# Row maxima of an attention unit: merged by one VectorE instruction, transposed in fp32, split into two fp16 parts behind the transpose

## What is computed

```python
xn = layernorm(x)
q, k, v = split(xn @ W_attn + b_attn)          # 16 heads of 16 channels
q, k = rope(q), rope(k)                        # here: over the head axis, 16 angles
att = softmax(where(causal, q @ k.T / 4, -inf))
s = (att @ v) @ W_proj + b_proj
h = silu(xn @ w_gate.T / 127) * (xn @ w_up.T / 127)
out = x + s * silu(h @ w_down.T / 127)
```

## Time and profile before

| | |
|---|---|
| median of 3 runs | 1229.83 us (1229.42 to 1235.92) |
| span of the profiled execution, first to last instruction | 1225.2 us |
| PE / DVE / ACT / POOL busy | 1124.7 / 1039.1 / 891.3 / 771.0 us |
| mean granted clock of PE | 0.993 of full speed |

### The profile page before, as it was taken

The page is one execution under the profiler, slowest core; times in us unless marked ns, Lnnn a source line. Parts: engine busy times, 40 slices in busy tenths (PEclk is TensorE's granted clock), DMA queues, the critical chain, the costliest instruction groups (busy, mean ns, idle before and its releaser), DMA issues.

```text
span 1225.2 us, 27668 instructions
## 1 busy us (share of the span) xinstructions
PE 1124.7 (92%) x9484; PEld 455.5 (37%) x9484; DVE 1039.1 (85%) x3124; ACT 891.3 (73%) x1708; POOL 771.0 (63%) x943
## 2 busy tenths in 40 slices
PE   3789989999999999999899999999999998999996
PEld 2223423434343443434334342333434343343433
DVE  6789889988989889989899888898898998989832
ACT  4457777777777777777677777777777786878774
POOL 3537445595837948298564966469483894737672
PEclk9989999999999999999999999999999999999999
DMA  6250042403242150611425033431516115240201
GB/s 174 74 147 12 12 123 76 120 28 114 54 146 57 28 150 22 169 29 53 125 71 133 23 99 68 121 83 28 141 32 171 30 32 146 69 93 18 62 2 52
DMA packets 71281, 97.51 MB, mean 80 GB/s; under 512 B 18398, under 2 KB 44388, under 8 KB 71140
## 3 DMA queue, kind: packets, MB, share of 16 engines
q1 hardware_dynamic: 71072, 95.73, 28.2%
q10 hardware_dynamic: 68, 0.01, 0.0%
HBM read 52.76 MB, written 34.47 MB: 71 GB/s over the span
## 4 chain that ended last, share of the span: by engine, by line
PE 50%; POOL 20%; DVE 14%; issue 6%; ACT 6%; DMA 2%; SPq 1%; POOLq 0%; DVEq 0%; ACTq 0%
PE ring L931 25%; PE acc L922 11%; PE st L871 7%; PE ring L898 5%; POOL xn L579 5%; POOL hf L1629 4%; DVE ring L1294 4%; POOL pexp L1599 3%; ACT pexp L1129 3%; DVE mx_a L1298 2%; POOL hT L1638 1%; DVE parts L1356 1%; POOL hT L1633 1%; POOL yn L1648 1%; PE ring L941 1%
## 5 line engine op out<-in xcount | busy, mean ns | idle before, releaser
L1129 ACT ACTIVATE pexp<-st 128x512 f32<-128x512 f32 x1152 | 624.1, 598 | 139.1 <-PE st L871 136.4
L1294 DVE CUSTOM_DVE_ANT_0 ring<-ring,tri 128x512 f32<-128x512 f32 (+3 forms) x1024 | 470.2, 522 | 40.5 <-PE ring L898 39.6
L1599 POOL TENSOR_SCALAR_AFFINE_SELECT pexp<-pexp 128x512 f32<-128x512 f32 x256 | 158.0, 635 | 341.8 <-ACT pexp L1129 250.8
L1298 DVE TENSOR_REDUCE mx_a<-ring 128x1 f32<-128x512 f32 x512 | 326.9, 682 | 28.1 <-PE ring L898 26.2
L922 PE MATMUL acc<-pexp,v_pad 128*17 128x512 f32 (+3 forms) x3072 | 304.3, 491 | 16.7 <-POOL pexp L1599 14.5
L898 PE MATMUL ring<-k_st,q_st 56*128 56x512 f16 (+4 forms) x1536 | 237.6, 326 | 32.9 <-DVE parts L1356 11.4
L871 PE MATMUL st<-q_st,k_st 58*128 58x512 f16 (+3 forms) x1536 | 234.8, 332 | 6.6 <-ACT pexp L1129 3.4
L871 PEld LDWEIGHTS st<-q_st,k_st 58*128 58x128 f16 x1536 | 61.9, 93 | 275.9 <-ACT pexp L1129 175.7
L1629 POOL TENSOR_TENSOR hf<-ga,ups 128x512 f32<-128x512 f32 x96 | 121.8, 1272 | 10.3 <-DVE ga L1365 8.8
L922 PEld LDWEIGHTS acc<-pexp,v_pad 128*17 128x17 f32 x3072 | 61.4, 96 | 154.6 <-issue 119.6
L1638 POOL TENSOR_TENSOR hT<-hf,hT 128x512 f16<-128x512 f32 x96 | 110.8, 1158 | 6.7
(11 more groups left out here) (155 smaller groups left out, 1430.6 us busy)
## 6 DMA issues: line engine op xcount, KB each, us to landing
parts_scratch<-parts SPq DMA_DIRECT2D x32, 512.0 KB, 3.0
q_st<-parts_scratch SPq DMA_DIRECT2D x62, 192.0 KB, 3.9
k_st<-parts_scratch SPq DMA_DIRECT2D x62, 192.0 KB, 4.4
parts_scratch<-parts SPq DMA_DIRECT2D x32, 256.0 KB, 3.6
xo<-in_x SPq DMA_DIRECT2D x32, 256.0 KB, 3.2
out<-xo SPq DMA_DIRECT2D x32, 256.0 KB, 2.3
xn<-in_x SPq DMA_DIRECT2D x7, 1024.0 KB, 8.1
yn<-yT SPq DMA_DIRECT2D x224, 32.0 KB
```

The lines of the kernel that those rows point to most:

```text
L1129: nc.scalar.activation(pexp[:, GH * (n % NSET) + j, :], st[:, (GH * n + j) % NST, :], ACT.Exp, scale=1.0 / (QK_SCALE * np.sqrt(D))).then_i ...
L1294: top_ = nc.vector.tensor_tensor_reduce(out=src, in0=src, in1=tri[:, CH - w:CH], scale=1.0, scalar=NEG, op0=ALU.add, op1=ALU.max, accum_ou ...
L1298: top_ = nc.vector.reduce_max(dst, src, AX.X)
L1599: nc.gpsimd.affine_select(out=t, in_=t, compare_op=ALU.is_ge, fill=0.0, base=0, pattern=[[0, GH], [1, P]], channel_multiplier=-1).then_inc ...
```

## The change

The pieces of a row's maximum now lie side by side in one tile, `mx_s`, whose second column POOL fills once with -3e38 in the prologue. One reduce over pairs (L1309 of the changed kernel) writes 32 fp32 maxima into `mx_m`. PE transposes these 32 columns in fp32. ACT copies the 32 rows out of PSUM with the scale -1/32768 to fp16, the high part (L1207), and then DVE forms the low part from the same bank and ACT's result (L1371), which frees the bank. SP's four DMAs take their rows from the new layout of `mT`. The fp16 identity and its two POOL instructions are gone.

```diff
@@ LAG @@
-    "vector": {"TX": 0, "QK": 0, "UPG": 0, "DN": 0, "FT": 0, "YT": 0, "LNS": 0, "BP": 0, "YR": 1},
+    "vector": {"TX": 0, "QK": 0, "UPG": 0, "DN": 0, "FT": 0, "YT": 0, "LNS": 0, "BP": 0, "YR": 1, "MT": 0},
@@ rows_of_maxima, issued by SP @@
-                    first = 2 * TT * (2 * a + part)
+                    first = 2 * TT * a
...
-                                  mT[first:first + 2 * TT, :]).then_inc(mrow_in[g], 16)
+                                  mT[first:first + 2 * TT, part, :]).then_inc(mrow_in[g], 16)
@@ PE, task MT @@
-                    pe.wait_ge(mp_chain, 3 * BY["MT"].at(kind, i, t))
+                    pe.wait_ge(mx_ready, BY["MT"].at(kind, i, t))
                     dst, ready = take(kind, i, t)
-                    nc.tensor.transpose(dst[0:2 * GH * TT, :].bitcast(fp16)[:, 0:P],
-                                        mx_p[:, :, :, :, :].rearrange("p a s j t -> p (a s j t)"), ident16[:, :])\
-                        .then_inc(ready, 1)
+                    nc.tensor.transpose(dst[0:GH * TT, 0:P], mx_m[:, :], ident[:, :]).then_inc(ready, 1)
@@ ACT, task MT @@
-                    nc.scalar.activation(mT[:, :], src[0:2 * GH * TT, :].bitcast(fp16)[:, 0:P], ACT.Copy)\
-                        .then_inc(ring_free[b], 1)
+                    nc.scalar.activation(mT[:, 0, :], src[0:GH * TT, 0:P], ACT.Copy, scale=-1.0 / M_UNIT)\
+                        .then_inc(mt_high, 1)
@@ DVE, split_maxima @@
                 wait_done(dve, *last_max(kind, i, t), 1)
-                nc.vector.tensor_tensor(m[:, :, :, 4:8], m[:, :, :, 4:8], mx_b[:, par, :, :, :], ALU.max)\
-                    .then_inc(mp_chain, 1)
-                dve.wait_ge(mp_chain, base + 1)
...
-                nc.vector.tensor_scalar(mx_p[:, :, 0, :, :], m, -1.0 / M_UNIT, None, ALU.mult).then_inc(mp_chain, 1)
-                dve.wait_ge(mp_chain, base + 2)
-                nc.vector.scalar_tensor_tensor(out=mx_p[:, :, 1, :, :], in0=m, scalar=-1.0 / M_UNIT,
-                                               in1=mx_p[:, :, 0, :, :], op0=ALU.mult,
-                                               op1=ALU.subtract).then_inc(mp_chain, 1)
+                nc.vector.tensor_reduce(mx_m[:, :].rearrange("p (r o) -> p r o", o=1),
+                                        mx_s[:, par, :, :, :].rearrange("p r t s -> p (r t) s"), AX.X, ALU.max)\
+                    .then_inc(mx_ready, 1)
@@ DVE, task MT @@
+                if t[0] == "MT":
+
+                    dve.wait_ge(mt_high, BY["MT"].at(kind, i, t))
+                    nc.vector.scalar_tensor_tensor(out=mT[:, 1, :], in0=src[0:GH * TT, 0:P], scalar=-1.0 / M_UNIT,
+                                                   in1=mT[:, 0, :], op0=ALU.mult, op1=ALU.subtract)\
+                        .then_inc(ring_free[b], 1)
@@ POOL, prologue @@
+                pool.memset(mx_s[:, :, :, :, :], NEG).then_inc(mx_clear, 1)
...
-                pool.memset(ident16[:, :], 0.0).then_inc(const0, 1)
...
-                pool.affine_select(out=ident16[:, :], in_=ident16[:, :], compare_op=ALU.not_equal, fill=1.0, base=0,
-                                   pattern=[[-1, P]], channel_multiplier=1).then_inc(const_ready, 1)
```

More of the change, by code:

```diff
@@ L423, in build_program @@
         ident = sb("ident", [P, P], fp32)
-        ident16 = sb("ident16", [P, P], fp16)
         tri = sb("tri", [P, CH], fp32)
@@ L444, in build_program @@
         yrec = sb("yrec", [P, 4, 4 * GH], fp32)
[L445 to L448, removed]
+        mx_s = sb("mx_s", [P, 2, GH, TT, 2], fp32)
+        mx_m = sb("mx_m", [P, GH * TT], fp32)
+        mT = sb("mT", [GH * TT, 2, P], fp16)
         hT = sb("hT", [P, 2, HID // P, CH], fp16)
@@ L524, in build_program @@
         stack_in = [sem(f"stack_in{g}") for g in range(GROUPS)]
-        mp_chain = sem("mp_chain")
+        mx_clear = sem("mx_clear")
+        mx_ready = sem("mx_ready")
+        mt_high = sem("mt_high")
         mrow_in = [sem(f"mrow_in{g}") for g in range(GROUPS)]
@@ L1285, in max_take @@
                     dve.wait_ge(tri_ready, 1)
+                    dve.wait_ge(mx_clear, 1)
                 for a in range(2):
@@ L1290, in max_take @@
                     for t, k0, w, p in found:
-                        dst = mx_b[:, par, a, p, t - 4:t - 3] if k0 else mx_a[:, par, a, p, t:t + 1]
+                        dst = mx_s[:, par, 2 * a + p, t, (k0 > 0):(k0 > 0) + 1]
                         src = ring[:, b, at:at + w]
@@ L1304, in split_maxima @@
                 par = t[1] % 2
-                base = 3 * (BY["MT"].at(kind, i, t) - 1)
-                m = mx_a[:, par, :, :, :]
                 wait_done(dve, *last_max(kind, i, t), 1)
-                nc.vector.tensor_tensor(m[:, :, :, 4:8], m[:, :, :, 4:8], mx_b[:, par, :, :, :], ALU.max)\
-                    .then_inc(mp_chain, 1)
-                dve.wait_ge(mp_chain, base + 1)
                 if kind != "pro":
                     wait_ready(dve, *mt_before(kind, i, t))
-                nc.vector.tensor_scalar(mx_p[:, :, 0, :, :], m, -1.0 / M_UNIT, None, ALU.mult).then_inc(mp_chain, 1)
-                dve.wait_ge(mp_chain, base + 2)
-                nc.vector.scalar_tensor_tensor(out=mx_p[:, :, 1, :, :], in0=m, scalar=-1.0 / M_UNIT,
-                                               in1=mx_p[:, :, 0, :, :], op0=ALU.mult,
-                                               op1=ALU.subtract).then_inc(mp_chain, 1)
+                nc.vector.tensor_reduce(mx_m[:, :].rearrange("p (r o) -> p r o", o=1),
+                                        mx_s[:, par, :, :, :].rearrange("p r t s -> p (r t) s"), AX.X, ALU.max)\
+                    .then_inc(mx_ready, 1)
             def stats(kind, i, p):
@@ L1696, in prologue @@
                 pool.memset(hf[0:64, 1, :], float(np.uint32(0x78007800).view(np.float32))).then_inc(k_const, 1)
-                pool.wait_ge(const0, 5)
+                pool.wait_ge(const0, 4)
                 for p in range(2):
```

## The result

| | before | changed |
|---|---|---|
| median of 6 runs each | 1229.62 us (1225.03 to 1235.92) | 1216.45 us (1214.25 to 1222.60) |
| ratio, 95% interval | | 0.9901 (0.9877 to 0.9924) |
| span of the profiled execution | 1225.2 us | 1215.5 us |

The changed kernel is faster by 1.0%, some 12 us. The forecast was 8.6 us and 1221.2, with a range of 1214.5 to 1230.5. The direction, the range and the place of the gain were right. The gain was larger than forecast: 1216.45 lies at the very edge of the forecast's own 1216 to 1225, and under the 1217.8 that the prediction gave for added work that costs nothing.

A forecast was written before the change was run, and what follows sets the result against it. PE (92% busy, 50% of the chain) bounds the kernel, so DVE gains count only where PE waits for DVE. -13.2 + 1.0 + 2.4 + 1.2 = -8.6 us, from 1229.8 to 1221.2; range 1214.5 to 1230.5.

The forecast's parts named there:

- The three instructions take turns with POOL: Slots 24 and 25: three small DVE instructions alternate with POOL's large ones, holding DVE 3.06 us; the reduce takes 0.22.
- -13.2 in slots 24 and 25: PE's wait at L898 for `parts` goes, 11.4 us, plus 6 x 0.30 us of idling in the products behind.
- DVE's wait for ACT in slot 25: Before L1371 DVE idles 0.9 us for ACT's copy; taken as no loss, at most 2.8 us.
- the rival that ended slower: L1371 waits for ACT in slots 7, 16 and 34, 24 times at about 1.1 us: 1246 us; chance 0.06.
- +1.0 for L1371 in slots 7, 16 and 34: L1371 delays DVE's maxima behind it by 0.2 to 0.3 us; between none and 6 us, taken as 1.
- +2.4 for the DMAs: SP issues the maxima's DMAs 0.85 us later; four uncovered places cost 0.6 us each, eight at slot 9 nothing.
- +1.2 in the prologue: DVE waits for ACT's copy and does L1371 before its next maxima, delaying PE's first scores: cost 1.2 us.
- The sum: -13.2 + 1.0 + 2.4 + 1.2 = -8.6 us on a span of 1225.2: 1216.6.
- From the span to the median: The median lies 4.6 us above the span, so 1229.8 - 8.6 = 1221.2.
- given back: Rival: slot 25 gets earlier but another part of the batch cannot follow, about half kept: 1227.8 us; chance 0.20.
- the reduce waits for POOL: Rival: in slot 24 the reduce still waits for POOL, gain some 6 us: 1228.4 us; chance 0.07.
- no gain: Rival: PE's idle time at L898 has another cause just behind `parts`: 1234.4 us; chance 0.05.

The follow-up runs named there:

- e3: Changed kernel with two more reduces of the same shape chained behind the reduce, results unread; 1216.58 us, ratio to before 0.9908.
- e2: Changed kernel with the old scaling and remainder put back behind the reduce on SBUF tiles, results unread; 1227.37 us, ratio to before 1.0007.
- e1: Changed kernel with a two-input tensor_tensor maximum in place of the reduce; 1217.45 us, ratio to before 0.9920.
- e8: The changed kernel as it is, run again beside later experiments; 1217.45 us, ratio to before 0.9882.
- e6: Changed kernel, but in the prologue DVE forms the low part one pair of maxima later; 1213.78 us, ratio to before 0.9869.
- e5: Changed kernel, but SP issues the high part's two DMAs when ACT is done, only the low part's behind DVE; 1213.16 us, ratio to before 0.9858.

## Why the prediction was right, and where its sizes were off

**The three instructions take turns with POOL.** Right, and shown: e3 and e2 differ only in the kind of the two added instructions, and 10.8 us lie between them. The reason that the prediction gave from the rows does not hold, though. It set the reduce apart because it reads one SBUF tile where L1309 reads two; but L1315 reads one as well and reached 1.22 us, and 1.25 in e2. By that reason the 0.22 was luck: it is the kind of the instruction that decides, as the rule cited beside it has it, and e3 was needed to see it. The Trainium skill (SBUF — State Buffer, "Who interferes with whom") says that tensor_reduce never takes part on trn2; the trace agrees, with 214 to 222 ns in 32 places, and in 64 more in e3. Its other rule (VectorE: DVE Perf Modes, "Rules for kernel authors"), which calls tensor_reduce the slowest VectorE operation and advises to consider restructuring, brings nothing at this place: alone the two-input merge of e1 is a little shorter, 0.19 us against 0.22, but beside POOL it takes 1.2, and e1 is not faster.

**-13.2 in slots 24 and 25.** The step was right: the wait of 11.4 is gone, and PE itself is what comes last. Measured are 14.4 us, or 13.9 without the place of lower clock in before: 2.07 in most batches, where 1.62 + 0.30 were counted. The rows of the two kernels show what was missed. A PE product starts before the one ahead has ended (886.95 against 887.11 in the changed kernel), so the idle times in brackets are too short by that overlap. L898 starts 2.02 us behind the scores in before (892.73 to 894.75) and 0.23 in the changed kernel (886.72 to 886.95); the next product starts 0.69 and 0.31 behind L898. That is 1.79 + 0.38 = 2.17 us a batch, not 1.92; 0.1 of it is lost again within these slots.

**DVE's wait for ACT in slot 25.** Forecast 0.9 us, measured 0.88, in six bodies, with no loss to be seen there. In slots 7, 16 and 34 DVE does not wait for ACT at all: the eight waits are six of slot 25, one of the prologue (3.7) and one of slot 25 in the last batch (0.4). So the rival that ended slower had no ground.

**+1.0 for L1371 in slots 7, 16 and 34.** Its duration was right, 0.272 us against 0.29. Its cost is not to be seen: the stretches from slot 7 to 16 and from slot 34 to 7 that have no late DMA agree with before within 0.1 us or are up to 0.3 shorter. That DVE's idle time covers it is likely and not shown.

**+2.4 for the DMAs.** That SP issues later was right: 0.79 us after ACT's end in slot 7, with 0.85 forecast. So was the cost where it was looked for: the forecast took four places at 0.6 us, those that waited before and do not lie at slot 9, and in these four PE idles 0.44 to 0.66 us, 2.2 in all, where it idled 0.3 before. What the forecast had at nothing is the rest. In the profiled execution PE visibly idles 6.6 us for these DMAs, in 9 places, in e8 4.6 in 7. At slot 9 PE is late by 0.10 to 0.15 us in six batches, not by up to 0.35, but by 0.5 and 2.1 in the two others; and two units that had not waited at all idle 0.3 and 1.5. These are single transfers that land late, which the forecast did not reckon with: most take 1.7 us from issue to landing, the slowest behind the 0.3, 1.5 and 2.1 took 3.7 to 3.9. The later issue had used up the slack, and which units pay is left to how the transfers land. Other stretches came out shorter, so that all stretches outside the start and slots 16 to 25 together are +2.2 us, or +3.3 without the place of lower clock in before, for this term and the one above, forecast at 3.4. That the total agrees is in part luck: the term above shows no cost, and the late transfers, with a place of lower clock behind one of them, fill its place.

**+1.2 in the prologue.** Right: +0.89 by the marks, +1.16 from the first transpose to the first scores (7.88 us before, 9.04 after), 1.0 won back by e6, and the row of L1371 shows DVE waiting in front of its maxima. The first scores were forecast near 77.0 and came at 78.53, because the profiled execution had lost 1.5 us before that, in a stretch that differs between executions of one kernel (below).

**The sum.** Without those 1.54 us of the start and the place of lower clock in before the marks give -13.9 + 0.9 + 3.3 = -9.7, against -8.6: 0.7 of the difference is the term of slots 24 and 25, 0.3 the prologue, and 0.1 the two terms of L1371 and the DMAs. The interval of the ratio, 9 to 15 us, holds it.

**From the span to the median.** The sum was carried over to the median by adding 4.6. In every run the time lies 1.7 us above that run's own span; the other 2.9 were there because the profiled execution of before was one of the quicker ones. That of the changed kernel was not: its 1217.2 lies above its median. So the two spans differ by 9.7 us and the two medians by 13.2, and the ratio with its interval is the better measure.

The rivals "given back", "the reduce waits for POOL" and "no gain" are excluded by the rows above: the saving of slots 24 and 25 stays in every batch that had the wait, the reduce is not stretched, and behind `parts` L898 has no other wait in these slots.

## What to carry to other kernels

A small VectorE instruction whose longest duration is several times its shortest is worth a look at what GpSimd does beside it: it may be paying for GpSimd's instructions, and each further one of its kind behind it pays again. A reduce over pairs in one SBUF tile did not pay here, and neither did an instruction with one of its inputs in PSUM; a tensor_scalar on one SBUF tile did, so the number of tiles read is not the sign to go by. And what matters is only what stands behind it that another engine needs. When work is moved behind a copy, let what needs only the copy go ahead, as the DMAs of the high part in e5.

## What the runs showed of the hardware

PE's clock at the start of the program differs between executions of the same kernel. Windows of the start (stretch, length, busy us and instructions of PE, PEld, DVE, ACT, POOL, then the granted clock, the DMA share and GB/s), first of before, then of the changed kernel, then of the changed kernel again (e8):

```profile
44.00:48.00 4.00, 2.69 (x13) 0.82 (x13) 3.34 (x6) 1.18 (x2) 1.16 (x2) 1.00 0.21 30
48.00:70.00 22.00, 17.20 (x101) 7.26 (x102) 18.67 (x59) 8.94 (x16) 11.76 (x10) 1.00 0.41 131
```

```profile
44.00:48.00 4.00, 2.94 (x10) 0.85 (x10) 2.48 (x4) 0.33 (x1) 1.50 (x2) 0.72 0.20 26
48.00:70.00 22.00, 17.69 (x100) 7.07 (x99) 17.16 (x55) 8.49 (x14) 10.26 (x9) 0.97 0.37 110
```

```profile
44.00:48.00 4.00, 2.32 (x10) 0.74 (x10) 2.48 (x4) 0.94 (x2) 2.12 (x2) 0.84 0.12 16
48.00:70.00 22.00, 18.29 (x87) 6.42 (x86) 16.72 (x54) 5.66 (x9) 8.85 (x7) 0.80 0.38 112
```

A share below 1.00 means that PE stood at the lower of its two levels, 1.2 GHz, for a part of the stretch. The first transpose of the maxima, which stands behind the same work in all of these kernels, came between 66.72 us (e5) and 72.42 (e8). The changed kernel alone has 69.49 and 72.42, so it differs without any edit. What decides it was not settled. The whole time goes with the mean clock: of the kernel before, seven runs beside e5 had spans of 1224.1 to 1228.7 at mean granted clocks of 0.989 to 0.993, and four had 1231.3 to 1235.2 at 0.985 to 0.988. Where in these runs the clock was lower is not on record; the traces of before and of the changed kernel each have one such place in the middle as well. Two kernels whose times differ by a few us are best compared over many runs, or from a mark behind the start.
